# DLRM tower on one core: eleven one-hot fields for thirteen, single lookup copies, three table buffers

## The chip, the core and the metric

The kernel runs on one core of a Trainium2 chip. The metric is the device time of one launch, in microseconds; the runs before gave 129.84 us as the median of three (129.02 to 130.34). The core has a matrix engine (TensorE, "PE" in the rows, with its weight loads as "PEld"), DVE (VectorE), ScalarE ("ACT"), GpSimd ("POOL") and SyncE ("SP", which only issues DMAs here). Each engine works through its own list of instructions in order, and waits at semaphores for the others.

## The reference

For 512 samples there is a dense vector of 128 numbers and 26 ids, one for each of 26 tables with rows of 128 numbers. Six tables have 1000 rows, eleven 1250, the others 12500 or 125000. All is fp32.

```python
e = stack([tbl_f[ids[:, f]] for f in range(26)], axis=1)      # 512 x 26 x 128
T = concatenate([dense[:, None, :], e], axis=1)               # 512 x 27 x 128
Z = einsum('bnd,bmd->bnm', T, T)                              # 27 x 27 dot products a sample
z = Z[:, iu0, iu1]                                            # the 351 pairs above the diagonal
h = concatenate([z, dense], axis=1)                           # 479 numbers
h = maximum(h @ W_top1 + b_top1, 0)                           # 512 wide ("layer 1")
h = maximum(h @ W_top2 + b_top2, 0)                           # 256 wide ("layer 2")
y = h @ W_top3                                                # 1 wide ("layer 3")
```

## The kernel before

The samples form four tiles of 128. All vectors go, transposed, into `XT`: 128 partitions (the vector's coordinate) x 512 samples x 32 places, so neighbouring samples lie 128 bytes apart and a sample's places next to each other. Place 0 is the dense vector, places 1 to 13 the fields of `ONEHOT`, places 14 to 26 the `GATHERED` fields, and places 27 to 31 are set to zero (L600).

**One-hot fields.** A small table is loaded whole (`table`, `TABLES` = 2 buffers, SP, L290; a load waits until the low part of the table two before it is made) and cut into chunks of 128 rows: 8 chunks for each of the first six fields, 10 for each of the other seven, 118 in all. The chunk times a one-hot matrix of 128 x 512 is the lookup. To keep fp32, the table is split into a high part (`t_hi`, a cast on ScalarE, L483, `high_part`) and a low part (`t_lo`, a subtraction on DVE, L578, `low_part`), and TensorE makes two products a chunk (L380 and L382). The one-hot matrices come in a ring of eight (`hot`): four of five are a comparison on DVE (L593), the fifth comes from ScalarE in two steps, a distance (L500) and a ReLU (L510). `hot_used` counts groups of up to four chunks that TensorE is through with; it frees the ring, the buffers of ids and the table parts. The high part of field i + 2 stands ahead of the first one-hot of field i + 1 in ScalarE's list. Lookups collect in PSUM (`work`, six banks), and after every third field one ScalarE copy moves three of them to `XT` (L534).

**Gathered fields.** GpSimd issues an indirect DMA for each tile and field (L331): 128 rows of a table go to `rows`, 13 for each tile, 52 in all, tile 0 first. TensorE transposes them in groups of four places (`GROUPS`; L366, the step "rows"), and ScalarE copies a group to `XT` (L548).

**Order.** `timeline` writes out `STEPS`, and TensorE, DVE and ScalarE each walk through that one list. `ROWS_AFTER` says after which one-hot field which groups are transposed: all of tiles 0 to 2 stand between or behind the one-hot fields; tile 3 comes later. Each waits for its own gathers only.

**Grams.** When all lookups are in `XT`, a half tile's step "gram" (L398) multiplies each sample's 27 x 128 matrix by itself, two samples a product. DVE and ScalarE copy two of four sample groups each (`copy_gram`): the low part to `Zlow` (L463), the high part to `Zt` (L470). The low parts get to their partitions of `Zt` by six small DMAs a tile (`low_stars`, L269 and L309), issued by SP; for the last tile GpSimd issues two of them (`SHARED_MOVES`).

**Layers.** Layer 1 of a tile is, for each of four blocks, a product with the dense vector (L342) and three with `Zt` (L348). fp32 products are two instructions each. DVE does the ReLU. Layer 2 (L442) has the weights as the stationary operand and is 8 products of 128 columns; DVE adds bias and ReLU (L626); layer 3 (L450) multiplies with `tail_sb`, and a copy (L630) and a DMA bring out a tile's results. Layer 1 of tile 2 stands behind the grams of tile 3.

The SP queue issues, in this order: the ids of tile 0 for the gathers, the ids of field 0, the tables and the broadcast ids of the fields (each with its wait), the dense vectors, `w1`, `w2`, the tail, then the moves and results.

## Time and profile before

| what | value |
|---|---|
| median of three runs | 129.84 us |
| profiled execution, own time | 131.07 us |
| its span, first to last instruction | 129.2 us |
| mean granted TensorE clock | 0.987 |
| TensorE busy | 109.3 us, 85% |
| DVE busy | 86.0 us, 67% |
| ScalarE busy | 77.2 us, 60% |
| GpSimd busy | 68.4 us, 53% |
| chain that ended last | PE 37%, POOL 36%, issue 9%, DMA 9% |

The busy shares are means over stages that differ: the one-hot stage ends near 78 us, the grams begin at 79.73 us. Matmuls are pipelined, so a TensorE instruction's printed duration is longer than its distance to the next. A bracket at the end of a row, like [2.09 <-ACT hot L510], says how long the engine was idle before and which instruction ended it.

### The profile page before, as it was taken

The page shows a single profiled execution, that of the slowest core. Times are in us where ns is not written, and L with a number is a line of the kernel's source. Part 1 is how long each engine was busy: PE and PEld are TensorE (multiplying, and loading weights), DVE is VectorE, ACT ScalarE, POOL GpSimd, SP SyncE. Part 2 cuts the span into 40 slices and gives each one's busy share as a digit, 9 for nine tenths or more (in the row PEclk, how much of TensorE's full clock was granted, in tenths as well). Part 3 has the DMA queues.
Part 4 walks back from the last instruction along what each step waited for, and adds up shares of the span by engine and source line. Part 5 has one row for each costly group of instructions (what it writes and reads, how often), then busy time and mean ns, then how long its engine had stood idle before and what let it go on. Part 6 is the DMA issues. An engine that isn't in the chain of part 4 may idle for free.

```text
span 129.2 us, 2741 instructions
## 1 busy us (share of the span) xinstructions
PE 109.3 (85%) x1032; PEld 92.8 (72%) x1032; DVE 86.0 (67%) x211; ACT 77.2 (60%) x166; POOL 68.4 (53%) x62
## 2 busy tenths in 40 slices
PE   5895799999993999999029996865879999999992
PEld 5863678788672888777027875865868997899980
DVE  4398889998988489979602666699423962295211
ACT  3383988996994987997105655699301944392001
POOL 2678888888888789889877778740000000003000
PEclk9999999999999999999976999999999999999999
DMA  4989967868867847579941212120000000000000
GB/s 107 238 240 284 316 217 255 235 215 274 295 210 163 257 110 240 147 256 217 393 131 41 61 41 61 46 73 12 16 8 0 10 16 3 5 0 21 5 0 0
DMA packets 7819, 16.86 MB, mean 130 GB/s; under 512 B 2466, under 2 KB 3390, under 8 KB 7678
## 3 DMA queue, kind: packets, MB, share of 16 engines
q1 hardware_dynamic: 5934, 13.06, 33.6%
q0 software_dynamic: 1728, 3.43, 9.4%
q10 hardware_dynamic: 144, 0.20, 0.5%
q8 instruction: 8, 0.13, 0.4%
q14 instruction: 5, 0.04, 0.1%
HBM read 16.44 MB, written 0.00 MB: 127 GB/s over the span
## 4 chain that ended last, share of the span: by engine, by line
PE 37%; POOL 36%; issue 9%; DMA 9%; DVE 4%; SPq 3%; ACT 1%; DVEq 0%; ACTq 0%
POOL rows L331 36%; PE work L398 8%; PE work L348 7%; PE work L442 6%; DMA rows<-tbl,idx 5%; PE work L380 4%; PE work L382 4%; PE work L342 3%; SPq L269 2%; DMA idx<-ids 2%; PE work L450 2%; PE tp L366 2%; DMA Zt<-Zlow 1%; DVE Zt L470 1%; DVE Zlow L463 1%
## 5 line engine op out<-in xcount | busy, mean ns | idle before, releaser
L331 POOL DMA_INDIRECT rows<-tbl,idx x52 | 66.5, 1278 | 18.0 <-issue 15.5
L593 DVE TENSOR_SCALAR hot<-ids_bc,rownum 128x512 fp32r<-128x512 int32 x95 | 41.0, 489 | 15.7 <-PE work L382 13.1
L380 PE MATMUL work<-hot,t_hi 128*128 128x512 f32 x118 | 48.3, 409 | 3.0 <-ACT hot L510 2.3
L382 PE MATMUL work<-hot,t_lo 128*128 128x512 f32 x118 | 46.7, 396 | 0.0
L380 PEld LDWEIGHTS work<-hot,t_hi 128*128 128x128 f32 x118 | 22.6, 191 | 10.9 <-ACT hot L510 4.4
L382 PEld LDWEIGHTS work<-hot,t_lo 128*128 128x128 f32 x118 | 22.6, 192 | 4.2
L578 DVE TENSOR_TENSOR t_lo<-table,t_hi 128x1280 fp32r<-128x1280 f32 (+3 forms) x15 | 17.9, 1198 | 0.6 <-ACT t_hi L483 0.6
L483 ACT CAST t_hi<-table 128x1280 fp32r<-128x1280 f32 (+3 forms) x15 | 15.4, 1028 | 4.6 <-DMA table<-small 4.6
L398 PE MATMUL work<-XT 128*64 128x52 f32 x512 | 16.2, 222 | 2.3 <-DVE Zt L470 1.3
L398 PEld LDWEIGHTS work<-XT 128*64 128x64 f32 x512 | 15.5, 138 | 3.3 <-issue 1.7
L500 ACT ACTIVATE apart<-ids_bc,minus_row 128x512 f32<-128x512 int32 x23 | 16.4, 715 | 1.9 <-DMA ids_bc<-ids_oh 1.9
L269 POOL DMA_DIRECT2D Zt<-Zlow x2 | 1.1, 554 | 30.8 <-DVE Zlow L463 30.8
L510 ACT ACTIVATE hot<-apart 128x512 fp32r<-128x512 f32 x23 | 14.5, 632 | 3.1 <-PE work L382 3.0
L548 ACT COPY XT<-tp 128x512 f32<-128x512 f32 (+1 forms) x16 | 8.1, 549 | 12.4 <-PE tp L366 12.4
L366 PE MATMUL tp<-ident,rows 128*128 128x128 f32 x52 | 7.8, 285 | 7.6 <-DMA rows<-tbl,idx 7.6
L470 DVE COPY Zt<-work 17x48 f32<-17x48 f32 (+1 forms) x64 | 12.8, 200 | 1.0
L463 ACT COPY Zlow<-work 14x224 f32<-14x224 f32 x16 | 5.7, 354 | 12.7 <-PE work L398 12.4
L470 ACT COPY Zt<-work 17x48 f32<-17x48 f32 (+1 forms) x64 | 12.5, 196 | 0.8
L366 PEld LDWEIGHTS tp<-ident,rows 128*128 128x128 f32 x52 | 6.4, 147 | 8.9 <-issue 8.1
L348 PE MATMUL work<-Zt,w_sb 128*128 128x128 f32 x84 | 11.5, 275 | 0.0
L534 ACT COPY XT<-work 128x1536 f32<-128x1536 f32 (+1 forms) x5 | 7.9, 1586 | 4.3 <-PE work L382 4.3
L348 PEld LDWEIGHTS work<-Zt,w_sb 128*128 128x128 f32 x84 | 10.4, 192 | 0.0
(34 smaller groups left out, 61.7 us busy)
## 6 DMA issues: line engine op xcount, KB each, us to landing
table<-small SPq DMA_DIRECT2D x7, 640.0 KB, 4.8
ids_bc<-ids_oh SPq DMA_DIRECT2D x13, 256.0 KB, 4.1
table<-small SPq DMA_DIRECT2D x4, 512.0 KB, 3.7
w_sb<-w SPq DMA_DIRECT2D x1, 1024.0 KB, 8.0
rows<-tbl,idx POOLq DMA_INDIRECT x52, 4.0
table<-small SPq DMA_DIRECT2D x2, 320.0 KB, 5.1
w_sb<-w SPq DMA_DIRECT2D x1, 512.0 KB, 8.1
dense_t<-dense SPq DMA_DIRECT2D x1, 256.0 KB, 5.5
```

The source lines that it names most:

```text
L331: nc.gpsimd.indirect_dma_start(rows[:, t, place - FIRST, :], None, tbls[f], bass.IndirectOffsetOnAxis(ap=idx[:, t, f:f + 1], axis=0)).then ...
L348: last = nc.tensor.matmul(l1_block(t, u), w1_sb[:, c, u * P:(u + 1) * P], Zt[:, t, c, :], start=False, stop=c == CHUNKS - 1)
L366: last = nc.tensor.transpose(tp[:, bank, j * P:(j + 1) * P], rows[:, t, a + j - FIRST, :], ident[:])
L380: nc.tensor.matmul(bank, t_hi[:, i % PARTS, c * D:(c + 1) * D], hot[:, k % HOTS, :], start=c == 0, stop=False)
L382: last = nc.tensor.matmul(bank, t_lo[:, i % PARTS, c * D:(c + 1) * D], hot[:, k % HOTS, :], start=False, stop=c == n - 1)
L398: last = nc.tensor.matmul(gr[PAD * s:PAD * (s + COUPLE), halves % HALVES, q, 0:COUPLE * FIELDS], XT[:, b:b + COUPLE, :].rearrange("d s n - ...
L470: last = copy(Zt[PAD * g:PAD * g + n, t, :, first:end:COUPLE], gr[PAD * s:PAD * s + n, half, :, column(s) + n - CHUNKS:column(s) + n].rear ...
L483: nc.scalar.copy(t_hi[:, i % PARTS, c0 * D:c1 * D], table[:, i % TABLES, c0 * D:c1 * D]).then_inc(hi_ready, 1)
L500: nc.scalar.activation(apart[:, j % 2, :], ids_bc[:, i % IDS, :], ACT.Abs, bias=minus_row[:, KINDS.index(OH_CHUNKS[i]), c:c + 1]).then_inc ...
L510: nc.scalar.activation(hot[:, k % HOTS, :], apart[:, j % 2, :], ACT.Relu, bias=1.0, scale=-1.0).then_inc(hot_act, 1)
L578: nc.vector.tensor_tensor(t_lo[:, i % PARTS, c0 * D:c1 * D], table[:, i % TABLES, c0 * D:c1 * D], t_hi[:, i % PARTS, c0 * D:c1 * D].bitcas ...
L593: nc.vector.tensor_scalar(hot[:, k % HOTS, :], ids_bc[:, i % IDS, :], rownum[:, v, c:c + 1], None, ALU.is_equal).then_inc(hot_dve, 1)
```

## The change

Two fields of 10 chunks each (15 and 18) leave `ONEHOT` and become gathered ones. 98 chunks remain in 11 fields, and each tile has 15 gathers, 60 in all, in groups of four, four, four and three places. Only the ids of the gathered fields go to `idx`, laid out on the host so that one DMA brings all four tiles.

The tables have three buffers. Each lookup is copied alone, one field later (after ScalarE's second one-hot of the next field), and the last one in two parts, 128 and 384 samples, of which the first gram needs the first. A lookup's bank is the field's number modulo six.

GpSimd's gathers get waits of their own (`row_turn`): from the sixth on, gather j waits until 3j - 14 chunks (at most 98) are used; some from 39 on also wait for a gram, a transposed group, a part of layer 1, or layer 2.

DVE sets the padding of `XT` to zero first of all; it copies the dense vectors behind field 8. Their DMA is issued after field 5's.

The order behind the one-hot fields changes: only tiles 0 and 1 have their rows in `XT` by then; rows of tile 2 come between the first grams and layers; layer 1 of tile 2 comes ahead of the grams of tile 3. The dense products are a step of their own ("dense"). Layer 2 of tiles 0 to 2 has the activations as the stationary operand and 4 products of 256 columns; its bias, ReLU and layer 3 are two DVE instructions with biases and weights broadcast to all partitions (`ends_sb`, one more DMA), and the result is a column. The last tile keeps its form, but layer 3 starts on its first half while the second is made. GpSimd issues three of the last tile's moves. The last tile's copies are ordered so that the second half's low part is copied before the first half's last high part. The gram products have 58 stationary columns for 64.

```diff
-ONEHOT = [4, 5, 6, 12, 16, 23, 2, 9, 11, 13, 14, 15, 18]
+ONEHOT = [4, 5, 6, 12, 16, 23, 2, 9, 11, 13, 14]
-TABLES = 2
+TABLES = 3
+CHUNKS_PER_ROW = 3
+CHUNKS_BEHIND = 14
+GRAMS_FIRST = {39: 1, 40: 2, 42: 3, 44: 4, 54: 5, 55: 6}
+TILE_ROWS_FIRST = {46: (2, 1), 50: (2, 2), 52: (2, 3), 59: (3, 0)}
+LAYER1_FIRST = {48: 1, 49: 2, 57: 3, 58: 4}
+LAYER2_FIRST = {51: 1}
-ROWS_AFTER = {3: [(0, 0), (0, 1)], 4: [(0, 2), (0, 3)], 6: [(1, 0), (1, 1)], 8: [(1, 2), (1, 3)], 10: [(2, 0), (2, 1)],
-              12: [(2, 2), (2, 3)]}
+DENSE_AFTER = 5
+COPIED_AFTER = 8
+ROWS_AFTER = {3: [(0, 0), (0, 1)], 5: [(0, 2)], 6: [(0, 3)], 7: [(1, 0)], 8: [(1, 1)], 10: [(1, 2), (1, 3)]}
-SHARED_MOVES = 2
+SHARED_MOVES = 3
...
-    steps += [("gram", 0, 0), ("gram", 0, 1), ("gram", 1, 0), ("gram", 1, 1), ("layer1", 0, 0),
-              ("layer1", 0, 1), ("layer2", 0, 0), ("gram", 2, 0), ("layer3", 0, 0),
-              ("gram", 2, 1), ("layer1", 1, 0), ("layer1", 1, 1), ("rows", 3, 0), ("rows", 3, 1), ("layer2", 1, 0),
-              ("rows", 3, 2), ("rows", 3, 3), ("layer3", 1, 0)]
-    steps += [("gram", 3, 0), ("gram", 3, 1), ("layer1", 2, 0), ("layer1", 2, 1), ("layer1", 3, 0), ("layer2", 2, 0),
-              ("layer1", 3, 1), ("layer3", 2, 0), ("layer2", 3, 0), ("layer3", 3, 0)]
+    steps += [("gram", 0, 0), ("gram", 0, 1), ("rows", 2, 0), ("gram", 1, 0), ("gram", 1, 1), ("rows", 2, 1),
+              ("dense", 0, 0), ("layer1", 0, 0), ("layer1", 0, 1), ("rows", 2, 2), ("layer2", 0, 0), ("rows", 2, 3),
+              ("gram", 2, 0), ("gram", 2, 1), ("dense", 1, 0), ("layer1", 1, 0), ("layer1", 1, 1),
+              ("rows", 3, 0), ("rows", 3, 1), ("layer2", 1, 0), ("rows", 3, 2), ("dense", 2, 0), ("layer1", 2, 0),
+              ("layer1", 2, 1), ("rows", 3, 3), ("gram", 3, 0), ("gram", 3, 1), ("layer2", 2, 0), ("dense", 3, 0),
+              ("layer1", 3, 0), ("layer2", 3, 0), ("layer3", 3, 0)]
...
+def chunks_first(j):
+    return min(j * CHUNKS_PER_ROW - CHUNKS_BEHIND, first_hot(K_OH))
...
-            sp.dma_start(idx[:, 0, :], ids[0:P, :]).then_inc(idx_in, 16)
+            sp.dma_start(idx[:], ids.rearrange("p (t f) -> p t f", t=TILES)).then_inc(idx_in, 16)
...
-                if i == HEADED - 1:
-                    sp.dma_start(idx[:, 1:TILES, :],
-                                 ids[P:BATCH, :].rearrange("(t p) f -> p t f", p=P)).then_inc(idx_rest_in, 16)
-            sp.dma_start(dense_t[:], dense).then_inc(dense_in, 16)
+                if i == DENSE_AFTER:
+                    sp.dma_start(dense_t[:], dense).then_inc(dense_in, 16)
...
+            def row_turn(j):
+                if 0 < chunks_first(j) and chunks_first(j - 1) < first_hot(K_OH):
+                    pool.wait_ge(hot_used, groups_used(chunks_first(j)))
+                if j in GRAMS_FIRST:
+                    pool.wait_ge(gram_full, GRAMS_FIRST[j])
+                if j in TILE_ROWS_FIRST:
+                    pool.wait_ge(tp_full, banks_filled(("rows", *TILE_ROWS_FIRST[j])))
+                if j in LAYER1_FIRST:
+                    pool.wait_ge(l1_part, LAYER1_FIRST[j])
+                if j in LAYER2_FIRST:
+                    pool.wait_ge(l2_full, LAYER2_FIRST[j])
...
+                        row_turn(t * len(GATHERED) + place - FIRST)
                         nc.gpsimd.indirect_dma_start(
...
-                    if i % LOOKUPS == 0 and lookup_group(i) >= 2:
-                        pe.wait_ge(lookup_copied, lookup_group(i) - 1)
-                    bank = lookup_banks(i)[:, i % LOOKUPS, :]
+                    if i >= LOOKUP_BANKS:
+                        pe.wait_ge(lookup_copied, i - LOOKUP_BANKS + 1)
+                    bank = lookup_bank(i)
...
-                        pe.wait_ge(lookup_copied, lookup_group(K_OH - 1) + 1)
+                        pe.wait_ge(lookup_copied, K_OH - 1)
+                        pe.wait_ge(last_copied, 1)
...
+                    if t == 1 and i == 0:
+                        pe.wait_ge(lookup_copied, K_OH)
...
+                elif kind == "layer2" and t < TILES - 1:
...
+                    for u in range(BLOCKS):
+                        last = nc.tensor.matmul(l2_block(t, 0), h1[:, u, :], w2_sb[:, u, :], start=u == 0,
+                                                stop=u == BLOCKS - 1)
...
+            def copy_lookups(i):
+                act.wait_ge(hot_used, groups_used(first_hot(i + 1)))
+                if i == K_OH - 1:
+                    nc.scalar.copy(XT[:, 0:P, 1 + i], lookup_bank(i)[:, 0:P]).then_inc(last_copied, 1)
+                    nc.scalar.copy(XT[:, P:BATCH, 1 + i], lookup_bank(i)[:, P:BATCH]).then_inc(lookup_copied, 1)
+                else:
+                    nc.scalar.copy(XT[:, :, 1 + i], lookup_bank(i)).then_inc(lookup_copied, 1)
...
-                    for k in mine_in(i)[1:]:
+                    for n, k in enumerate(mine_in(i)[1:]):
                         one_hot(k)
+                        if n == 0 and i:
+                            copy_lookups(i - 1)
+                    if i and len(mine_in(i)) < 2:
+                        copy_lookups(i - 1)
...
+            nc.vector.memset(XT[:, :, PLACES:PAD], 0.0).then_inc(xt_ready, 1)
             dve.wait_ge(iota_ready, len(KINDS))
...
+                    if i == COPIED_AFTER:
+                        dve.wait_ge(dense_in, 16)
+                        nc.vector.tensor_copy(XT[:, :, 0], dense_t[:]).then_inc(dense_copied, 1)
...
-                        nc.vector.memset(XT[:, :, PLACES:PAD], 0.0).then_inc(xt_ready, 1)
...
+                    if t == TILES - 1 and i == 1:
+                        copy_high(nc.vector.tensor_copy, t, 0, (halves - 1) % HALVES, second).then_inc(gram_dve, 1)
...
+                elif kind == "layer2" and t < TILES - 1:
...
+                    nc.vector.tensor_tensor(h2_sum_sb[:], l2_block(t, 0), ends_sb[:, 0, :], ALU.add).then_inc(h2_sum, 1)
+                    dve.wait_ge(h2_sum, t + 1)
+                    nc.vector.scalar_tensor_tensor(out=h2_part[:], in0=h2_sum_sb[:], scalar=0.0, in1=ends_sb[:, 1, :],
+                                                   op0=ALU.max, op1=ALU.mult,
+                                                   accum_out=y_column[:, t:t + 1]).then_inc(y_ready, 1)
```

## Rows read from the trace of the kernel before

**Rows 1.** Chain of waits, 56 to 72 us: start, duration, what.
```profile
59.86 6.94 DMA rows<-tbl,idx
...
71.75 0.23 PE work L380
```

**Rows 2.** TensorE's instructions in time, 10 to 70 us: start, duration, form, [idle before].
```profile
13.63 0.50 PE L380 MATMUL work<-hot,t_hi 128*128 128x512 f32 x1 [2.09 <-ACT hot L510]
...
41.19 0.63 PE L366 MATMUL tp<-ident,rows 128*128 128x128 f32 x4 [2.04 <-DMA rows<-tbl,idx]
41.57 0.47 PE L380 MATMUL work<-hot,t_hi 128*128 128x512 f32 x1
...
66.94 1.09 PE L366 MATMUL tp<-ident,rows 128*128 128x128 f32 x4 [5.61 <-DMA rows<-tbl,idx]
```

**Rows 3.** Busy time by engine in one stretch; the granted clock is third from last.
```profile
67.00:68.00 1.00, 1.00 (x5) 1.00 (x6) 0.00 (x0) 0.00 (x0) 0.79 (x1) 0.50 0.29 66
```

**Rows 4.** GpSimd's instructions in time.
```profile
3.86 1.15 POOL L331 DMA_INDIRECT rows<-tbl,idx  x1 [2.42 <-DMA idx<-ids]
...
21.60 2.02 POOL L331 DMA_INDIRECT rows<-tbl,idx  x1 [0.30 <-issue]
...
49.93 2.07 POOL L331 DMA_INDIRECT rows<-tbl,idx  x1 [0.30 <-issue]
...
62.24 1.79 POOL L331 DMA_INDIRECT rows<-tbl,idx  x1 [0.30 <-issue]
...
84.94 0.94 POOL L331 DMA_INDIRECT rows<-tbl,idx  x1 [0.30 <-issue]
```

**Rows 5.** DVE's instructions in time.
```profile
5.42 0.49 DVE L593 TENSOR_SCALAR hot<-ids_bc,rownum 128x512 fp32r<-128x512 int32 x1 [2.14 <-DMA ids_bc<-ids_oh]
...
21.49 1.22 DVE L578 TENSOR_TENSOR t_lo<-table,t_hi 128x1024 fp32r<-128x1024 f32 x1
...
57.17 1.48 DVE L578 TENSOR_TENSOR t_lo<-table,t_hi 128x1280 fp32r<-128x1280 f32 x1
58.57 3.25 DVE L593 TENSOR_SCALAR hot<-ids_bc,rownum 128x512 fp32r<-128x512 int32 x8
...
77.39 2.19 DVE L600 MEMSET XT<- 128x2560 f32 x1 [0.45 <-issue]
```

**Rows 6.** Landing of the gathers, from 20 to 64.3 and 64.3 to 86 us.
```profile
DMA to landing us min/median/max: 2.7/5.0/7.2
...
DMA to landing us min/median/max: 2.5/2.6/3.2
```

**Rows 7.** Chain of waits from the first gram to the end.
```profile
79.27 0.44 ACT XT L548
79.73 2.09 PE work L398 x64
...
84.45 0.38 DVE Zlow L463
...
89.14 1.68 DMA Zt<-Zlow
...
102.62 0.67 PE work L348 x6
...
124.22 2.00 PE work L442 x16
...
127.47 0.28 DVE y L630
```

**Rows 8.** Instructions grouped by line and shape: count, busy us, mean ns, idle before.
```profile
L534 ACT COPY XT<-work 128x1536 f32<-128x1536 f32 x4 | 6.9, 1728 | 2.1 <-PE work L382 2.1
...
L534 ACT COPY XT<-work 128x512 f32<-128x512 f32 x1 | 1.0, 1019 | 2.2 <-PE work L382 2.2
```

**Rows 9.** ScalarE's instructions in time.
```profile
57.08 0.64 ACT L510 ACTIVATE hot<-apart 128x512 fp32r<-128x512 f32 x1
...
58.23 1.25 ACT L483 CAST t_hi<-table 128x1280 fp32r<-128x1280 f32 x1
```

More of the change, by code:

```diff
@@ L169, in hots_made, with dlrm_tower @@
     return sum(by_scalar(x) == scalar for x in range(k + 1))
-def dlrm_tower(nc, dense, ids, ids_oh, tbls, small, w1, w2, tail, out):
+def dlrm_tower(nc, dense, ids, ids_oh, tbls, small, w1, w2, tail, ends, out):
     f32, f32r, i32 = mybir.dt.float32, mybir.dt.float32r, mybir.dt.int32
@@ L348, in from_pairs @@
                     last = nc.tensor.matmul(l1_block(t, u), w1_sb[:, c, u * P:(u + 1) * P],
-                                            Zt[:, t, c, :], start=False, stop=c == CHUNKS - 1)
+                                            Zt[:, t, c, :], start=False,
+                                            stop=c == CHUNKS - 1 and (t == TILES - 1 or u == BLOCKS - 1))
                 return last
@@ L670 @@
     dlrm_tower(nc, aps["dense"], aps["ids"], aps["ids_oh"], {f: aps[f"tbl_{f}"] for f in GATHERED},
-               [aps[f"small_{i}"] for i in range(K_OH)], aps["w1"], aps["w2"], aps["tail"], out)
+               [aps[f"small_{i}"] for i in range(K_OH)], aps["w1"], aps["w2"], aps["tail"], aps["ends"], out)
     r = run(nc, [arrays], core_ids=[0])
```

194 lines of the change are left out of this document (100 added, 94 removed).

## The prediction

> **What bounds the kernel now.** I read four views in this order: the chain of waits, TensorE's instructions in time, GpSimd's instructions in time, and then the two engines that feed the one-hot products.
>
> Until shortly before 79 us TensorE multiplies one-hot chunks, two products each at 0.23 us [rows 1], so 0.46 us a chunk. That stretch has three holes. The tenth chunk waits 2.1 us for ScalarE's one-hot; ScalarE makes it behind the cast of table 2, whose load had waited for a free table buffer. The other two are waits for gathered rows, 2.0 and 5.6 us [rows 2]. After the long one the clock was granted at 0.5 of full speed, the 1.2 GHz level [rows 3]; by 71.75 a product took 0.23 us again. The chain of waits goes through this last hole: all gathers of GpSimd up to the one at 59.86, then its landing [rows 1].
>
> GpSimd starts its first gather at 3.86 us, the 35th at 62.24 and the 52nd and last at 84.94 [rows 4]. So the first 34 steps take (62.24 - 3.86) / 34 = 1.72 us each, the last 17 take 22.7 / 17 = 1.34. One alone takes 0.95 us and 0.30 of gap, 1.25. The slow ones are those that meet DVE's subtraction for the low table part: the gather at 21.60 takes 2.02 us beside the subtraction at 21.49 [rows 4, 5]. The excess over 1.25 us is 58.4 - 42.5 + 22.7 - 21.3 = 17.3 us in all. Landing, counted from the start, has a median of 5.0 us while tables stream in and 2.6 later [rows 6].
>
> After the first gram product (G, 79.73), three things set the time: the order of the steps, the gram copies (the first gram is ready at 81.8, the second half's low copy follows at 84.45, so 2.6 us a half tile), and the moves of the low part, which land at 90.82 or G + 11.1 [rows 7].
>
> **The change part by part.**
>
> *Two one-hot fields fewer.* 20 of 118 chunks go: 20 x 0.46 = 9.2 us of TensorE on the path. 8 gathers and 8 transposes come; four transposes take 0.4 us (41.19 to 41.57) [rows 2], so 0.8 us.
>
> *Three table buffers.* Table 2's load needn't wait for a release, but queues behind the loads in flight. Between 0 and the 2.1 us of the wait, I take 1.4 us, because ScalarE still has to cast table 2 ahead of that one-hot.
>
> *Single lookup copies.* Copies of three lookups took 1.73 us in the mean, 0.58 a lookup; the only single one took 1.02 [rows 8]. Eleven cost 6.3 to 11.2 us; I take 11.2, the row of the same shape. A ten-chunk field on ScalarE is then two one-hots with their distances at 58.23 - 57.08 = 1.15 each, a cast at 1.25, a lookup at 1.02 and a row copy at 0.44: 5.0 us [rows 7, 9]. TensorE needs 4.6 and 0.4 for transposes, 5.0. DVE needs eight comparisons at 3.25 / 8 and a subtraction at 58.57 - 57.17 = 1.40, 4.65 [rows 5]. The three stand level: the copies hide behind TensorE with no slack, and I allow 1 us for ScalarE being late.
> A single copy writes one fp32 number every 128 bytes. The Trainium skill, SBUF — State Buffer ("Door 1: The DMA port swizzle"), says that an access pattern needs at least two hits in a 16-byte line for full bandwidth; by it every element of a single copy pays, which speaks against this part. The trace agrees in kind, 1.02 us against 0.58.
>
> *Memset first.* Its 2.19 us move from just ahead of the grams to DVE's start. The hole of 2.14 us ahead of the first comparison covers it [rows 5], and what it lacks lies in DVE's wait for the row numbers before. Were the ids early, it would delay the first chunk by up to 2.2 us. The dense copy moves behind field 8: under 1 us on DVE, against 0.35 us of slack a field.
>
> *TensorE up to G.* Tenth chunk at 12.2; 89 chunks at 0.46, 41 us; 30 transposes, 3 us: 56.2. With the 1 us for ScalarE and the copy of the last lookup, G is 58.
>
> *Gathers.* All ids come in one DMA, so the start stays near 3.9. Each gather j from the sixth on waits for chunk 3j - 14. A gather takes 1.7 us and three chunks 1.4, so it finds them done; the waits for grams, transposes and layers from j = 39 on are for things over 5 us old by this sum. Nothing but GpSimd's own work is queued behind them. The excess falls with the subtractions (15 to 13, 0.87) and comparisons (95 to 79, 0.83): 0.85 x 17.3 = 14.7 us. The last of 60 starts at 3.9 + 59 x 1.25 + 14.7 = 92.3 and lands at 94.9.
>
> *After G.* Layer 1 of tile 0 waits for the moves until 11.2 and, without its dense part, takes 4 x 0.67 = 2.7 [rows 7]: 13.9. Layer 2 of tiles 0 to 2 turns its operands round, 4 products of 256 columns for 8 of 128. One lies between a 128-column product (2.00 / 8 = 0.25, two instructions) and two instructions of 512 columns (0.46), the four between 1.0 and 1.8 us; I take 1.4. With transposes, copy and ReLU the grams of tile 2 start at 17.0, end at 21.0; dense part 0.9 and layer 1 to 24.6; transposes 0.8 and layer 2 to 26.8; transposes and dense part to 28.1; layer 1 to 31.0; the last rows' transposes and copy to 31.9. Without a wait for rows that is 58 + 31.9 = 89.9. Bias, ReLU and layer 3 of those tiles become two DVE instructions of 256 columns in DVE's idle time; if that cover went they would cost about 1 us a tile. But the rows land at 94.9, and with 0.9 for transposes and copy the last grams start at 95.8: the gathers bind by 6 us.
>
> *The end.* From the last tile's grams: 4.0 for two halves, 0.8 for low copies. The six moves took 5.6 us from there; now SP has three and GpSimd three, so half of the 3.9 of issuing and the landing of 1.7: 3.7. Layer 1 2.7, layer 2 2.0, and the 1.5 us from 126.22 to the end of the y copy at 127.75, less 0.2 for the halves of layer 3 waiting apart. 14.5 in all, then 1.45 until the span ends [rows 7].
>
> **Sum.** 95.8 + 14.5 + 1.45 = 111.8 us of span against 129.2: 17.4 less. The profiled execution took 131.07 us, 1.2 more than the median of 129.84. So 113.7 on its own scale and 112.4 on that of the median.
>
> **The rivals.**
>
> *Gathers don't bind.* The end is 89.9 + 14.5 + 1.45 = 105.9 of span, 106.5 on the median. It needs an excess of 9 us for the 14.7. Against it: slow gathers come with the subtractions. For it: a TensorE that is late leaves DVE idle, which speeds GpSimd. Chance 0.2.
> The Trainium skill, SBUF — State Buffer ("Who interferes with whom"), says that `tensor_tensor` takes only the read side of the shared ports and that descriptor generation needs the write side, marked as inferred. By it the subtractions would slow no gather and this rival would come; the gather of 2.02 us in this trace speaks against it.
>
> *The clock falls in the tail, or gathers are slower.* The rows for the third-last transposes come some 3 us after TensorE is ready. The hole of 5.6 us was followed by 1.2 GHz. If 3 us are too, dense part, layer 1 and some of a gram (4 to 5 us) take twice as long: 117. A one-hot stretch at 1.8 us a gather, for 1.72, adds 3 to 4 us. Chance 0.2.
>
> *Three buffers do nothing.* The tenth chunk comes at 13.6 still, G is 59.4, and the end doesn't move, since the gathers bind. Chance 0.15, within the forecast.
>
> *Slower than before.* GpSimd's queue has 60 gathers in place of 52, and the last tile's rows stand at its end. It decides once the last gather starts 17.4 us later, at 109.7: (109.7 - 3.9) / 59 = 1.79 us each over all 60. From the 29th to the 35th (49.93 to 62.24) a gather took 2.05; at that pace throughout the last would start at 125, and the median be 145. Against: the excess needs DVE's one-hot work, which ends near 56 us, and then 1.34 holds. Chance 0.03.
>
> **How the numbers follow.** Forecast 0.56, gathers not bound 0.2, clock or contention 0.2, no change 0.01, slower 0.03. Under 1% can't be told from no change here. The range takes in the rival without the bound at its lower end, 106.5, and the clock at its upper, 117.5. Faster by over 1% 0.96, within 1% 0.01, slower 0.03.
>
> **What would show it.** Right: GpSimd busy until about 93 us with no longer gap; TensorE's waits ahead of transposes of tile 3; G at 57 to 60; single copies at 1.0 us; no long wait ahead of the tenth chunk. Wrong: gaps on GpSimd that TensorE's releases end (its new waits bind), G after 63, subtractions that slow no gather, or a granted clock of 0.5 beyond 60 us.

## The result and the profile after

The changed kernel takes 120.36 us (four runs, 117.16 to 123.88) where the kernel before, beside it, takes 130.09: a ratio of 0.908 with an interval of 0.892 to 0.924. Faster, as forecast, but 8 us above the 112.4 of the forecast and outside its range. Its profiled execution took 122.29 us, with a span of 120.5, and was one of its slower ones; the same kernel profiled again took 117.03, with a span of 115.2. Both are shown; the readings below rest on what both have, or on the second.

TensorE in time, first profile of the changed kernel (start, duration, form, idle before):

```profile
12.26 0.50 PE L400 MATMUL work<-hot,t_hi 128*128 128x512 f32 x1 [0.70 <-ACT hot L539]
...
44.45 0.63 PE L386 MATMUL tp<-ident,rows 128*128 128x128 f32 x4 [1.80 <-DMA rows<-tbl,idx]
...
53.22 0.63 PE L386 MATMUL tp<-ident,rows 128*128 128x128 f32 x4 [3.57 <-DMA rows<-tbl,idx]
...
111.41 2.44 PE L367 MATMUL tp<-Zt,w_sb 128*128 128x128 f32 x12 [1.77 <-DMA Zt<-Zlow]
```

The second profile:

```profile
43.52 0.63 PE L386 MATMUL tp<-ident,rows 128*128 128x128 f32 x4 [1.25 <-DMA rows<-tbl,idx]
50.66 0.63 PE L386 MATMUL tp<-ident,rows 128*128 128x128 f32 x4 [1.93 <-DMA rows<-tbl,idx]
62.70 3.51 PE L421 MATMUL work<-XT 128*58 128x52 f32 x123
90.48 0.63 PE L386 MATMUL tp<-ident,rows 128*128 128x128 f32 x4 [1.63 <-DMA rows<-tbl,idx]
93.23 0.63 PE L386 MATMUL tp<-ident,rows 128*128 128x128 f32 x4 [0.40 <-DMA rows<-tbl,idx]
95.51 2.92 PE L367 MATMUL work<-Zt,w_sb 128*128 128x128 f32 x24 [0.75 <-DMA Zt<-Zlow]
99.32 3.62 PE L421 MATMUL work<-XT 128*58 128x52 f32 x128 [0.57 <-ACT XT L593]
107.77 1.57 PE L367 MATMUL tp<-Zt,w_sb 128*128 128x128 f32 x12 [1.91 <-DMA Zt<-Zlow]
112.99 0.38 PE L479 MATMUL work<-h,tail_sb 128*1 128x128 f32 x2 [0.21 <-ACT h L605]
```

Against [rows 2] the wait ahead of the tenth chunk shrank from 2.09 to 0.70 us. The 5.61 us for the rows of tile 2 are gone, since those rows are no longer wanted there, and two waits for the rows of tile 1 have come. The first gram (G) stood at 79.73 [rows 7] and is at 65.25 in the first profile, 62.70 in the second; the forecast had 58. The last grams begin at 102.44 and 99.32, for 95.8.

Windows of the first profile (columns: time, busy of five engines, granted clock, DMA share, GB/s):

```profile
54.00:56.00 2.00, 2.00 (x6) 1.61 (x5) 0.54 (x2) 2.00 (x4) 1.48 (x2) 0.50 0.21 53
84.00:86.00 2.00, 2.00 (x82) 2.00 (x80) 0.79 (x3) 0.81 (x3) 1.39 (x3) 1.00 0.84 54
112.00:114.00 2.00, 2.00 (x11) 2.00 (x11) 0.29 (x1) 0.05 (x1) 0.00 (x0) 0.50 0.02 0
```

and of the second:

```profile
52.00:54.00 2.00, 2.00 (x7) 1.52 (x6) 0.88 (x2) 2.00 (x3) 1.55 (x2) 0.50 0.23 67
80.00:85.00 5.00, 4.43 (x135) 4.13 (x134) 2.69 (x11) 2.34 (x9) 3.78 (x4) 1.00 0.49 50
85.00:90.00 5.00, 3.85 (x35) 3.61 (x33) 3.59 (x14) 3.30 (x14) 3.78 (x4) 1.00 0.63 42
```

Behind the hole of 3.57 us in the first profile and that of 1.93 in the second the clock is granted at 0.50, the 1.2 GHz level. In the kernel before it fell behind the hole of 5.6 us [rows 3] and stayed at 1.00 behind those of 2.09 and 2.04. In the tail it falls behind the 1.77 us of the first profile and not behind the 1.91 of the second, so the length of a hole alone doesn't decide it. In the first profile it is also low from 91 to 94 us; there TensorE had stood still for 1.7 us between 87 and 90 us, for nothing that the profile names. And between 80 and 90 us the DMA engines are busy for half the time and more (0.49 and 0.63 of it in the second profile) while they move only 42 to 50 GB/s, which is what eight gathers bring.

GpSimd in time, first profile, then DVE in time:

```profile
33.44 3.47 POOL L350 DMA_INDIRECT rows<-tbl,idx  x1 [0.30 <-issue]
```

```profile
33.72 1.48 DVE L623 TENSOR_TENSOR t_lo<-table,t_hi 128x1280 fp32r<-128x1280 f32 x1
```

GpSimd, second profile: the 1st, 23rd, 30th and last gather, then the landings of those issued from 20 to 57, 57 to 80 and 80 to 90 us:

```profile
4.31 1.15 POOL L350 DMA_INDIRECT rows<-tbl,idx  x1 [2.87 <-DMA idx<-ids]
...
43.63 1.79 POOL L350 DMA_INDIRECT rows<-tbl,idx  x1 [0.30 <-issue]
...
54.91 0.94 POOL L350 DMA_INDIRECT rows<-tbl,idx  x1 [0.31 <-issue]
...
92.75 0.94 POOL L350 DMA_INDIRECT rows<-tbl,idx  x1 [0.30 <-issue]
```

```profile
DMA to landing us min/median/max: 2.5/5.3/7.2
...
DMA to landing us min/median/max: 2.5/2.6/3.4
...
DMA to landing us min/median/max: 3.7/4.4/5.6
```

The last gather starts at 92.75, where the forecast put it at 92.3, and no gap of GpSimd's is longer than 0.31 us: the new waits bind nowhere here. But the pace is uneven: (43.63 - 4.31) / 22 = 1.79 us for each of the first 22 and (92.75 - 54.91) / 30 = 1.26 at the end. The landing of the last tile's rows, 2.6 us before [rows 6], is 4.4.

The gathers that run beside one of DVE's subtractions are the slow ones: by the second profile's rows 18 of the 60 do, and they take 1.62 us in the mean (up to 2.68); the other 42 take 1.01 (up to 1.28).

The wait of 1.93 us at 50.66 was for the 23rd gather. The chain of waits has its landing:

```profile
43.63 6.89 DMA rows<-tbl,idx
```

SP issued the load of the weights at 42.67, one microsecond before that gather.

Groups by line, first profile (count, busy us, mean ns, idle before); then DVE in time:

```profile
L350 POOL DMA_INDIRECT rows<-tbl,idx x60 | 74.5, 1242 | 21.1 <-issue 15.5 <-DMA idx<-ids 2.9 <-PE work L402 1.5
...
L551 ACT COPY XT<-work 128x512 f32<-128x512 f32 x10 | 11.1, 1110 | 0.0
```

```profile
1.35 2.19 DVE L611 MEMSET XT<- 128x2560 f32 x1 [1.35 <-PEq L695]
```

### The profile page after: what moved, and what is told of

The parts are those of the page before. It is cut to its first block, busy times and chain, and to the rows that moved or that the text cites. A ratio compares the mean times of both kernels' runs of the same rounds, so it can differ in the third digit from the quotient of the medians.

```text
span 120.5 us, 2570 instructions
## 1 busy us (share of the span) xinstructions
PE 102.5 (85%) x964; PEld 87.3 (72%) x964; DVE 75.4 (63%) x193; ACT 73.4 (61%) x163; POOL 77.0 (64%) x71
## 4 chain that ended last, share of the span: by engine, by line
PE 50%; DMA 16%; POOL 13%; issue 9%; DVE 5%; SPq 4%; ACT 1%; DVEq 0%; ACTq 0%
POOL rows L350 13%; PE work L367 10%; PE work L400 10%; PE work L402 10%; DMA rows<-tbl,idx 10%; PE work L421 7%; PE tp L386 3%; SPq L272 3%; PE work L460 3%; DMA Zt<-Zlow 3%; DMA idx<-ids 3%; PE tp L367 2%; DVE Zlow L491 2%; PE work L361 2%; PE work L470 1%
## 5 line engine op out<-in xcount | busy, mean ns | idle before, releaser
L350 POOL DMA_INDIRECT rows<-tbl,idx x60 | 74.5, 1242 | 21.1 <-issue 15.5
L400 PE MATMUL work<-hot,t_hi 128*128 128x512 f32 x98 | 40.3, 411 | 1.2 <-ACT hot L539 0.7
L638 DVE TENSOR_SCALAR hot<-ids_bc,rownum 128x512 fp32r<-128x512 int32 x79 | 33.5, 482 | 9.8 <-PE work L402 9.7
L402 PE MATMUL work<-hot,t_lo 128*128 128x512 f32 x98 | 39.3, 401 | 0.0
L400 PEld LDWEIGHTS work<-hot,t_hi 128*128 128x128 f32 x98 | 19.0, 194 | 7.2 <-ACT hot L539 1.1
L402 PEld LDWEIGHTS work<-hot,t_lo 128*128 128x128 f32 x98 | 19.0, 194 | 3.6
L421 PE MATMUL work<-XT 128*58 128x52 f32 x512 | 14.7, 217 | 2.2 <-ACT XT L593 1.1
L421 PEld LDWEIGHTS work<-XT 128*58 128x58 f32 x512 | 14.1, 133 | 3.1 <-ACT XT L593 1.6
L529 ACT ACTIVATE apart<-ids_bc,minus_row 128x512 f32<-128x512 int32 x19 | 13.7, 721 | 1.7 <-DMA ids_bc<-ids_oh 1.7
L491 DVE COPY Zlow<-work 14x224 f32<-14x224 f32 x16 | 6.1, 381 | 13.7 <-remote 4.6
L551 ACT COPY XT<-work 128x512 f32<-128x512 f32 x10 | 11.1, 1110 | 0.0
```

The costliest lines, as they stand in the source:

```text
L350: nc.gpsimd.indirect_dma_start(rows[:, t, place - FIRST, :], None, tbls[f], bass.IndirectOffsetOnAxis(ap=idx[:, t, place - FIRST:place - F ...
L400: nc.tensor.matmul(bank, t_hi[:, i % PARTS, c * D:(c + 1) * D], hot[:, k % HOTS, :], start=c == 0, stop=False)
L402: last = nc.tensor.matmul(bank, t_lo[:, i % PARTS, c * D:(c + 1) * D], hot[:, k % HOTS, :], start=False, stop=c == n - 1)
L421: last = nc.tensor.matmul(gr[PAD * s:PAD * s + COUPLED, halves % HALVES, q, 0:COUPLE * FIELDS], XT[:, b:b + COUPLE, :].rearrange("d s n -> ...
L491: return copy(Zlow[:, t % 2, :, first:end:COUPLE], gr[PAD * s:PAD * s + LOW, half, :, column(s):column(s) + LOW].rearrange("n q m -> n m q"))
L529: nc.scalar.activation(apart[:, j % 2, :], ids_bc[:, i % IDS, :], ACT.Abs, bias=minus_row[:, KINDS.index(OH_CHUNKS[i]), c:c + 1]).then_inc ...
```

## Experiments

The experiments form five sets. Times of different sets are compared only by their ratio to the kernel before, which was timed beside each set: it took 131.0 us in the first set, 139.35, 130.36, 139.02 and 129.9 in the others. The changed kernel was timed again in three of them. The question is where the 3.4 us of the second profile's span (115.2 for 111.8) and the further 5.3 of the first go. Theory P says that DVE's subtractions hold up the gathers, so that the rows of tile 1 come late, and that the clock falls behind the hole. Rivals are a long landing beside tables and weights, the third table buffer, the waits of GpSimd, and, for the end, the column store among the last gathers.

### First set: the kernel again, no subtraction, later weights, two buffers

**The changed kernel once more.**

> The changed kernel as it is, for an interval and another profile. Theory P (pace): gathers that meet DVE's subtractions go at about 1.96 us each up to the 23rd, rows of tile 1 come late, TensorE stands still and its clock falls after the holes. Expected again: first gram near 65 us, last gather starting near 96 us, span 115 to 120. Rival L (landing): the pace is a side matter, the rows are late because three table buffers and weights loaded from 43 us fill the DMA queues (landing 5 to 6 us for 4 to 5). Both expect the same here; if the stop of all engines near 88 to 90 us of the first profile is no property of the kernel, it is absent.

Measured: 119.07 us (116.52 to 121.98). Its profile is the second one above.

**A reduction for the subtraction.** The low part of the tables is left out: TensorE multiplies the high part twice, and DVE spends as long on one input.

```diff
-nc.vector.tensor_tensor(t_lo[...], table[...], t_hi[...].bitcast(f32), ALU.subtract)
+nc.vector.tensor_reduce(apart_max[...], table[...], mybir.AxisListType.X, ALU.max)
```

> The low table part is left out: DVE runs a reduction over the same table part (one SBUF input, about the same 1.2 to 1.5 us) in place of the subtraction (two SBUF inputs), and both products of a chunk use the high part. DVE's and TensorE's time stay. Theory P: slow gathers of 2 to 3.5 us disappear, pace 1.3 us, the holes at rows of tile 1 go, first gram at 57 to 59 us, 6 to 8 us less time. Rival L, or if any busy DVE slows a gather: pace and first gram stay within 1.5 us.

Measured: 114.2 us (112.14 to 114.53) for the 119.07 of the changed kernel, whose fastest run is 116.52. The forecast had 6 to 8 us; it is 4.9. DVE in time and GpSimd in time, at the place of the pair shown above:

```profile
33.18 1.48 DVE L624 TENSOR_REDUCE apart_max<-table 128x1 f32<-128x1280 f32 x1
```

```profile
32.89 1.19 POOL L351 DMA_INDIRECT rows<-tbl,idx  x1 [0.30 <-issue]
34.74 1.62 POOL L351 DMA_INDIRECT rows<-tbl,idx  x1 [0.66 <-PE work L403]
36.66 1.05 POOL L351 DMA_INDIRECT rows<-tbl,idx  x1 [0.30 <-issue]
```

An instruction of the same 1.48 us that reads one operand doesn't hold the gather up: 1.19 us for 3.47. The 23rd gather starts at 36.66 for 43.63, no wait for rows is left in the one-hot stage, and G comes at 57.41 for 62.70. All 60 gathers together take 63.2 us for the 71.4 of the second profile. This is P. The end moved by less than G, since TensorE then stood still for 3.36 us ahead of 83.04, for nothing that the profile names, some us after the store of its first column at 75.42. What the forecast weighed (the Trainium skill, SBUF — State Buffer, "Who interferes with whom", infers that `tensor_tensor` leaves descriptor generation alone) is measured by this too: `tensor_tensor` does slow the gathers here, against that inference.

**The weights' load later.** The loads of `w1`, `w2`, the tail and the broadcast ends wait until TensorE is through with 88 of the 98 chunks; they are issued from 51.91 us on.

```diff
+            sp.wait_ge(hot_used, groups_used(first_hot(K_OH - 1)))
```

> Weights, tail and broadcast ends are issued only when 88 chunks are used (about 57 us), not at 43 us. Rival L: the gather of the last row of tile 1's second group lands some 2 us earlier, the hole of 3.6 us ahead of it shrinks to under 2, the clock does not fall there, 2 to 4 us less time. Theory P: at most 1 us less, as the gather starts no earlier. Weights must be in by 74 us; if they land after that, time is lost there.

Measured: 117.27 us, ratio 0.9105 [0.9015, 0.9195]. The 23rd gather starts at 42.08 and lands in 3.2 us for the 6.89. The holes of tile 1 in mid-stage go, but its last rows now meet the weights (landing 5.5 to 6.6 us), and TensorE waits 3.60 us for them at 60.45. G is 61.25 for 62.70. So the landing beside the weights has a part in the holes that P alone doesn't have: moving the big load moved the hole. No time is gained over the changed kernel, whose range (116.52 to 121.98) holds this one's (117.16 to 120.66).

**Two table buffers.**

> TABLES back to 2, all else as changed. If the third buffer only starts table 2 earlier, the tenth chunk comes at 13.6 us for 12.3 and the time is 0 to 1.4 us longer. Rival L: fewer tables in flight, gathers land about 1 us earlier in the first 30 us, rows of tile 0 and 1 come earlier, and the time is equal or up to 2 us shorter.

```diff
-TABLES = 3
+TABLES = 2
```

Measured: 117.38 us (115.62 to 119.39). The tenth chunk comes at 13.64 behind 2.01 us of waiting, 1.4 us later than with three, as the forecast took it. There is no hole at the rows of tile 1, G is 58.80, and the end isn't later. The subtractions are whole here, yet the 23rd gather starts 3.4 us earlier than the 43.63 with three buffers:

```profile
40.27 1.59 POOL L350 DMA_INDIRECT rows<-tbl,idx  x1 [0.30 <-PE work L402]
```

The weights are issued at 43.98, so this gather is well ahead of them; it lands in 5.8 us. The third buffer gains 1.4 us early on and doesn't bring it to the end. Why the first 22 gathers lose less to the subtractions with two buffers (6.4 us over 0.95 each, for 10.0) isn't shown; the subtractions fall at other times against the gathers. The third set has the pair again.

### Second set: the store, the rows, the waits

The raised DMA share between 80 and 90 us begins with the first column store, 128 pieces of 4 bytes, which SP issues at 81.16 in the second profile. The changed kernel sends a tile's results behind the next tile's moves. In the first of these kernels the results of all tiles are sent behind the last tile's moves; in the second, rows of tiles 0 and 1 are transposed up to two fields later; the third has none of GpSimd's new waits.

```diff
-                if t:
-                    result(t - 1)
-            result(TILES - 1)
+            for t in range(TILES):
+                result(t)
```

> The results of tiles 0 to 2 are stored behind the last tile's moves, not between the moves. Theory S (stores): in all profiles of the changed kernel the DMA share jumps from about 0.25 to 0.6 to 1.1 at an unchanged 50 GB/s some 2 us after the first store of a result column (128 pieces of 4 bytes) and stays up for 8 us; gathers issued then land after 4 to 6.5 us for 2.6, and rows of tile 3 are late. Without the store there the share stays at 0.25, landing at 2.6, the last tile's first gram starts 2.5 to 4 us after less than 34 us from the first gram (36.6 in the last profile), 2 to 4 us less time. Rival G (gathers and moves alone fill the engines, or the column form of layer 2 has nothing to do with it): the share rises at 80 to 90 us all the same and the time is unchanged.

```diff
-ROWS_AFTER = {3: [(0, 0), (0, 1)], 5: [(0, 2)], 6: [(0, 3)], 7: [(1, 0)], 8: [(1, 1)], 10: [(1, 2), (1, 3)]}
+ROWS_AFTER = {3: [(0, 0)], 4: [(0, 1)], 6: [(0, 2)], 7: [(0, 3)], 9: [(1, 0)], 10: [(1, 1), (1, 2), (1, 3)]}
```

> Transposes of gathered rows move behind later one-hot fields: first groups of tile 0 behind fields 3 and 4, then 6 and 7, tile 1 behind 9 and 10. Theory P: TensorE stands 3 to 7 us at rows of tile 1 because gathers are at 1.8 to 1.95 us each; with the later places the holes ahead of transposes inside the one-hot stage go, no clock fall at 50 to 57 us, first gram at 59 to 61 us for 62.7 to 65.3, and 1 to 3 us less time, as far as the gathers of tile 3 don't hold it. Rival: rows are late at any place (landing grows with a busy DVE and TensorE), first gram stays at 62 or later.

```diff
-                        row_turn(t * len(GATHERED) + place - FIRST)
```

> GpSimd's waits before its gathers are taken out. They were forecast to bind nowhere; the gaps between gathers were 0.30 us. Expected: same time within 1%, gaps of 0.30 us. Rival: the waits kept gathers apart from the table loads or from the grams, and without them it is 1 to 3 us faster or slower.

Stores and rows late together:

> Both edits, stores late and rows late. If both theories hold, the gains add as far as gathers allow: last gather near 92 us, last tile's first gram near 95.5, span 110 to 112, time 112 to 114. If the gathers' pace alone holds the end, it is no better than the stores alone.

Measured: 131.42 us, ratio 0.9371 [0.9274, 0.9468]; 131.44, 0.9421 [0.9314, 0.9529]; 150.45, 1.0884 [1.0784, 1.0984]; 130.89, 0.9401 [0.9311, 0.9492]. The whole set was slower, and the kernel without waits became slower than the kernel before. Its grams, grouped:

```profile
L420 PE MATMUL work<-XT 128*58 128x52 f32 x512 | 22.7, 234 | 31.4 <-issue 30.3 <-ACT XT L592 1.1
```

and in time:

```profile
82.13 0.24 PE L420 MATMUL work<-XT 128*58 128x52 f32 x1 [2.56 <-issue]
...
98.96 2.34 PE L420 MATMUL work<-XT 128*58 128x52 f32 x41 [0.36 <-issue]
```

TensorE waited 30.3 us in its grams for nothing that the profile shows ("issue"), again and again between 62 and 99 us, and ran freely from 98.96 on, 6.3 us after GpSimd's last gather (92.71). I read it as TensorE's own instructions coming late beside the gathers' traffic; that is argued, not shown. What is shown: the other three kernels of this set, which have GpSimd's waits, stand still in the same way for 6.2 to 11.8 us only, while those waits hold GpSimd for 10 to 13 us. So the waits that the forecast called idle guard against this. With the rows late alone the first column store is issued at 92.76, and the DMA share from 95 to 100 us is 0.60; with the stores late it is 0.15. With the rows late alone, no wait for rows is left in the one-hot stage and G is 59.45, as that forecast had it; with both edits a wait of 2.44 us at 60.45 is back. What either is worth in time can't be told under the stalls.

### Third set: the same questions where the grams run freely

The changed kernel:

> The changed kernel beside the three others, since the last four ran where the kernel before took 139 us for 131. Theory F (fetch): TensorE's grams, 128 short instructions in 4 us, run out of instructions while gathers are in flight; there they stood 0.4 to 2.6 us at a time on nothing that the profile shows, until the gathers ended. Where the kernel before takes 129 to 131 us: 117 to 119 us and hardly such gaps; where it takes 137 or more: 130 to 133 and 6 to 15 us of them.

Without the waits:

> No waits before the gathers. Theory F: where the grams starve, 15 to 20 us slower than the changed kernel of this call; where they don't, within 1.5% of it, as gathers already ran with gaps of 0.30 us. Rival W (the waits cost or save nothing of their own, the slow run was the chip): equal to the changed kernel in this call, wherever it runs.

Stores and rows late:

> Stores late and rows late, against the changed kernel of this call. Theories P and S together: first gram 1 to 4 us earlier, DMA share no longer up at 80 to 90 us, rows of tile 3 land after 2.6 us, 2 to 4 us less time (ratio 0.97 to 0.985). If the end is held by the gathers' pace alone: less than 1 us.

The same with two table buffers:

> As the one before it, with two table buffers for three. The tenth chunk comes 1.4 us later. If more tables in flight slow the gathers (landing 5.6 us for 4.4 in the first 20 us), it is equal or up to 1.5 us faster than the same with three; if not, 0 to 1.4 us slower.

Measured: the changed kernel 121.18 us, ratio 0.9432 [0.9301, 0.9563]; without waits 120.27, 0.9162 [0.8933, 0.9392], and no stall in the grams, so here the waits decide nothing that can be told (the profile without waits does have TensorE standing still for 5.9 us in all between 83.6 and 90.5 us, for nothing that it names; the DMA share there is at first 0.95, behind the column store at 79.25); stores and rows late 118.38 (112.89 to 119.36); with two buffers 117.69, 0.9008 [0.8822, 0.9194]. No run with stores and rows late and three buffers is as slow as the fastest of the changed kernel here (119.47). The landing of the gathers issued from 80 to 90 us, first in the changed kernel, then with stores and rows late:

```profile
DMA to landing us min/median/max: 3.4/5.5/6.1
```

```profile
DMA to landing us min/median/max: 2.4/2.6/3.3
```

The landing is back at 2.6 us, and the DMA share of 80 to 95 us at 0.20 to 0.26. But one gather beside a subtraction took 4.36 us, and the last one started at 95.30 for 91.70. TensorE waited 2.38 us at 94.19 for a gather that started at 91.56 and landed in 2.5, and the last grams began at 99.29. So with the landing mended the slow gathers bind. Whether the store or the later rows mended it isn't told apart here; the fifth set has the one without the other.

The pair with three and two buffers comes out as in the first set: with three the 23rd gather starts at 43.96 and TensorE waits 2.43 us for rows ahead of G, with two it starts at 40.15 and no wait for rows is left there. So with whole subtractions the third buffer has a part in the holes, in both pairs of profiles. In time neither pair can be told apart.

### Fourth set: one cause at a time

The changed kernel, and then the stores late alone:

> The changed kernel as the measure for the three others of this call. 117 to 121 us, DMA share up at 80 to 90 us, a first gram at 61 to 65 us, last gather starting at 92 to 93.

> Only the stores of the result columns move behind the last tile's moves. Theory S: DMA share stays at 0.2 to 0.26 from 80 to 95 us, gathers land after 2.6 us, ratio to the changed kernel of this call 0.97 to 0.985, and no stop of all engines there. Rival G: the end hangs on the gathers' pace alone, then the last gram starts no earlier and the ratio is 0.99 to 1.0.

The stores late, and work for TensorE ahead of the last layer 1, while it waits for the moves:

```diff
+KEEP = 16
...
+                    for _ in range(KEEP):
+                        nc.tensor.transpose(l1[:, 1, :], ident[:], ident[:])
```

> Stores late, and 16 transposes into an unused PSUM part ahead of the last tile's layer 1, where TensorE stood 1.8 us. Theory C (clock): after that hole the clock is granted at 0.5 for some 3 us in about half of the profiles, which costs 1.3 to 1.7 us; with the transposes it stays at 1.00 from the last gram to the end, and the median is 0.5 to 1.5 us under stores late alone. Rival: the transposes run into the end of the wait and cost 0 to 0.5 us, with the clock no different.

The stores late, and each subtraction from the third table on in two halves a few comparisons apart (the first half is shown):

```diff
+                nc.vector.tensor_tensor(t_lo[:, i % PARTS, c0 * D:m * D], table[:, i % TABLES, c0 * D:m * D],
+                                        t_hi[:, i % PARTS, c0 * D:m * D].bitcast(f32), ALU.subtract)
+                HALF_DONE[i, c0] = m
...
```

> Stores late, and each subtraction of a table from the third on in two halves with two comparisons between. Theory P: a gather is held up for the length of the DVE instruction that it meets, so slow gathers take 1.6 us for 2 to 3.5, the last starts 3 to 5 us earlier (88 to 90), and 1 to 4 us less time than stores late alone. Rival D (a gather is held up by DVE having no gap at all, however it is cut): the same starts and time within 1 us; DVE has one instruction more a table, 0.1 us each.

Measured: 130.88, ratio 0.9431 [0.9391, 0.9471]; 130.32, 0.9362 [0.9282, 0.9443]; 129.71, 0.9270 [0.9187, 0.9352]; 126.26, 0.9016 [0.8962, 0.9070]. Halving is worth 4 us over the late stores alone, with an interval that touches none of the others. Its G is 57.84 with no wait for rows ahead of it; the three others have 61.01, 64.45 and 60.50, each with such waits. The grams stalled in this set too, 6.7 to 10.6 us, and the forecasts of absolute times and of the last gather failed with them: the changed kernel was to take 117 to 121 us. The late stores took the DMA share from 95 to 100 us from 0.62 to 0.17, but the gain in time, forecast at 1.5 to 3%, can't be told (0.6 us in the medians). The last layer 1 of the kernel with the stores late (its second part, and the clock in the last window):

```profile
118.79 1.71 PE L366 MATMUL tp<-Zt,w_sb 128*128 128x128 f32 x12 [1.89 <-DMA Zt<-Zlow]
120.29 2.77 PE L366 MATMUL work<-Zt,w_sb 128*128 128x128 f32 x12
...
121.00:123.00 2.00, 2.00 (x11) 2.00 (x11) 0.29 (x1) 0.00 (x0) 0.00 (x0) 0.50 0.00 0
```

and of the one with transposes ahead of it:

```profile
118.71 1.57 PE L367 MATMUL tp<-Zt,w_sb 128*128 128x128 f32 x12
120.12 1.50 PE L367 MATMUL work<-Zt,w_sb 128*128 128x128 f32 x12
...
121.00:123.00 2.00, 2.00 (x20) 2.00 (x19) 0.64 (x2) 0.28 (x1) 0.00 (x0) 1.00 0.00 0
```

A hole of 1.89 us was enough for the clock to go to 1.2 GHz; the same products took 2.77 us for 1.50. The forecast had the median 0.5 to 1.5 us lower; the difference of 0.6 us is within the intervals.

### Fifth set: all three causes taken away

> The changed kernel with three edits at once: a tile's results are sent one tile later, each subtraction of a table's low part is made in two halves a few comparisons apart, and 16 transposes of the unit matrix stand ahead of the last layer 1. If the three causes are separate (gathers held up by subtractions, a landing stretched by the early store, the clock in the tail), they add: no hole of over 1 us ahead of the transposed rows in the one-hot stage, first gram near 59, rows of the last tile landed under 4 us after issue, a last layer 1 at full clock, and a span of some 111 where the changed kernel has 115 to 117 beside a kernel before of 130; where the kernel before takes 139, as it did for the kernels with one edit alone, 124. If the gains are one and the same stretch of time (the last gathers would hold the end anyway), no more than the halves alone gave, a ratio of 0.90 to the kernel before.

> The same three edits, and two table buffers as in the kernel before. If the third buffer has no part in the end: the tenth chunk 1.4 us later, first gram up to 1 us later, the end within 1 us of the kernel with three buffers. If it costs something (table loads that stand in the gathers' way), 1 to 2 us faster than that.

Both kernels have the store edit as above: all results behind the last tile's moves, not one tile later as the first of these texts says.

Measured: **111.1 us** (110.85 to 112.68), ratio 0.8704 [0.859, 0.8818]; with two buffers 112.2 (111.55 to 113.17), 0.8777 [0.8676, 0.8877]. TensorE in time in the first:

```profile
58.09 3.62 PE L421 MATMUL work<-XT 128*58 128x52 f32 x128
...
87.27 0.63 PE L386 MATMUL tp<-ident,rows 128*128 128x128 f32 x4 [0.37 <-DMA rows<-tbl,idx]
...
92.37 3.62 PE L421 MATMUL work<-XT 128*58 128x52 f32 x128 [0.57 <-ACT XT L595]
...
100.81 1.58 PE L367 MATMUL tp<-Zt,w_sb 128*128 128x128 f32 x12
...
106.03 0.38 PE L481 MATMUL work<-h,tail_sb 128*1 128x128 f32 x2 [0.21 <-ACT h L607]
```

its last gather, a window, and the landing of the gathers issued from 80 to 90 us:

```profile
88.37 0.95 POOL L350 DMA_INDIRECT rows<-tbl,idx  x1 [0.30 <-issue]
...
80.00:85.00 5.00, 4.93 (x51) 4.66 (x45) 4.13 (x17) 3.79 (x17) 3.78 (x5) 1.00 0.26 63
...
DMA to landing us min/median/max: 2.5/2.5/3.3
```

G is at 58.09, the DMA share is 0.26, the rows land in 2.5 us, the clock of the whole execution is 1.00. The span is 109.3 us for the expected 111. This kernel beats the changed one as well as the kernel before: its ratio's interval ends at 0.8818, and the changed kernel's intervals begin at 0.892, 0.930 and 0.939 (they stem from other sets). The rows of tiles 0 and 1 stand where the change put them, so later rows aren't what mended the landing. That it is the store is borne out by where the share rises in the other profiles: behind a first column store at 75.42 it is 0.59 from 75 to 80 us, behind one at 77.39 it is 0.77 from 80 to 85, behind those at 92.8 it is 0.60 and 0.62 from 95 to 100. Taken away together the three causes give back the whole miss; what each is worth alone was timed only in the stalled fourth set. Of the two kernels here the one with three buffers is ahead by 1.1 us in the medians, with intervals that overlap, and its first gram comes 0.6 us earlier (58.70 with two): with the subtractions halved, the third buffer makes no holes.

## Why the prediction came out too low

The direction was right, and so was the gain of the one-hot stage: 20 chunks less, the long hole gone, the grams earlier, no gaps on GpSimd. What was not right is the path behind it: the forecast let the last gather bind the end, and in the profiles TensorE's own chain did. The number was 8 us too low, for steps of the sum that the runs price.

**The step that failed first is "TensorE up to G".** It summed chunks and transposes with no wait for the rows of tile 1, though the forecast's own pace of gathers (1.72 us) and landing (5.0 us) stood beside it: by these the 30th and last gather of tile 1 would start at 3.9 + 29 x 1.72 = 53.8 and land at 58.8, after TensorE's 56.2. By the second profile the first 22 took 1.79 each, the 23rd started at 43.63, 1.9 us after the 41.7 of that pace, and landed beside the weights in 6.89 us, 1.9 more than the 5.0. TensorE waited 1.25 and 1.93 us and then worked at 1.2 GHz for some 3 us. G came at 62.70, and at 65.25 in the first profile, for 58. With the subtractions halved and nothing else done to this stage, G is 58.09, and 57.84 in the fourth set. So the term was right for a stage without holes, and what was missing is 4.7 to 7.3 us that sit in the holes and behind them. Slow gathers are a shown cause, and not the only one: weights loaded later and two table buffers took these two holes away as well, with the subtractions whole. Pace, landing and the time of the weights' load meet in one due time, and their shares weren't timed apart. The forecast had the price of the subtractions, 14.7 us over all gathers, and used it only for the last gather.

**The second is the landing of the last tile's rows**, 2.6 us by [rows 6]. It was measured from 64.3 us on, behind all table loads and with no store of columns. The change puts a column store of tile 0 there, 128 separate pieces of 4 bytes, and the landing became 4.4 us in the median (5.2 in the first profile, 5.5 in the third set). SP's four moves took 6.39 us for 3.12 with the store late, and layer 1 of tile 2 waited 0.75 for them:

```profile
86.40 6.39 SPq L272 DMA_DIRECT2D Zt<-Zlow  x4
```

The second profile's chain of waits runs through these moves and this layer 1 to the last grams, so even with the rows in time they would have held them. A forecast that counts "a result is a column" as nothing but two DVE instructions misses that the DMA counts too.

**The third is a rival that came true in part**: the clock falls in the tail. It was given 4 to 5 us at the third-last rows. It came instead in the one-hot stage and, in the first profile, from 91 to 94 us and at the last layer 1: from the start of the last grams to the last product 15.8 us for 13.7.

Two of the forecast's signs of being wrong came in the first profile: a first gram after 63 us, and a granted clock of 0.5 beyond 60 us.

**What was right.** The last gather, in the second profile: 92.75 for 92.3, an excess of 92.75 - 4.31 - 59 x 1.25 = 14.7 us, the forecast's number; it is 96.14 in the first. It didn't set the time: its rows were in when TensorE came to them at 98.26. The end, from the last grams to the end of the span: 115.2 - 99.32 = 15.9 us for 15.95. The tenth chunk at 12.26 for 12.2. Three buffers gave the 1.4 us taken. The memset lies at 1.35 to 3.54, ahead of the ids: DVE takes up its work behind them at 5.56, for 5.42 before. Single copies take 1.11 us for 1.02. GpSimd's new waits bound nowhere in the changed kernel of the first and third sets; in the variants of these sets the longest gap that TensorE ended was 0.66 us.

**What else was off by a little.** In the fastest kernel, with nothing in its way, the last grams stand 92.37 - 58.09 = 34.3 us behind G, for 31.9 in the forecast. Two layer 2 lie in that stretch, and each takes 1.9 us (95.92 to 97.80 in its trace) for 1.4, just above the bound of 1.8: 1.0 us. The moves of tile 0 let layer 1 start 11.9 us behind G for 11.2: 0.7. The remaining 0.7 is spread over transposes and copies. So the rival "gathers don't bind" has come in that kernel (nothing waits for the last rows), and the span is 109.3 where the rival had 105.9.

**The sum by these parts**, for the second profile. G is 4.7 late. The chain behind it takes 36.6 us (99.32 - 62.70), 2.3 more than the 34.3: about what the waits of 1.63, 0.40 and 0.75 us come to, less the 0.37 that the fastest kernel has there (2.4). So the last grams stand at 58.0 + 4.7 + 34.3 + 2.3 = 99.3, and TensorE's chain holds them, not the gathers. With 15.9 behind them that is the span of 115.2. The forecast had 3.5 us to spare between such a chain (92.3) and its 95.8, since it let the gathers bind; the miss in the last grams is 7.0 less these 3.5. So a bound that didn't bind hid half of what was missing from TensorE's chain; that the miss isn't 7 us is luck. The first profile has G 2.6 us later than that, the last grams 3.1 later (the stop of 1.7 us and the low clock from 91 to 94 lie there, in place of the waits for rows) and 2.2 more behind them, its span of 120.5.

## What to carry to other kernels

Where an instruction slows another engine's queue, put the slower pace into every consumer's due time, not only into the last one's. Count a result's pieces before you call its store free: a column of 128 words of 4 bytes beside gathers isn't free. A hole of 1.8 to 1.9 us in front of a matrix product can cost 1.4 to 2.1 us more, through the clock; find something for TensorE to do in it, or close it.

## What the runs showed of the hardware

- A subtraction of two table operands (1.48 us) stretched a gather from 0.94 to 3.47 us, in two profiles to 4.36 and 4.37; a reduction of one operand of the same length left it at 1.19. Halved and spread apart, 58 of 60 gathers took 0.94 to 1.68.
- In the grams TensorE can stand still with no releaser in the profile: in every profile of the second and fourth set (30.3 us without GpSimd's waits, 6.2 to 11.8 with them) and in none of the other three. The kernel before took 139 us in those two sets for 130. The same kernel shows it in one set and not in another, and the first and the fourth set ran on the same chip; what decides it stays open.
- Outside the grams TensorE stood still without a releaser for 1.7, 4.1 and 5.9 us in three of the profiles with an early column store, from 4 us behind that store on; in no profile of the first, third and fifth sets with the store late. That the store causes it is not shown.
- The column store among gathers raised the DMA share from 0.25 to 0.49 and 0.63 for 10 us, with no more bytes moved.
- TensorE's clock was granted at 1.2 GHz behind holes of 1.77, 1.89, 1.93 and 3.57 us, and was not behind 1.88 in the fourth set, 1.91 in the second profile, and 2.04 and 2.09 in the kernel before.
